# A fused cross-attention and FFN block of two layers: P turned by DMA in steps 75 to 123, and four orders changed

## What is computed

```python
x = x + tanh(g_xattn[0]) * attn(layernorm(x), ctx, mask, L0 weights)
x = x + tanh(g_ffn[0])   * mx_ffn(layernorm(x), w_gate, w_up, w_down)
x = x + tanh(g_xattn[1]) * attn(layernorm(x), ctx, mask, L1 weights)
x = x + tanh(g_ffn[1])   * (layernorm(x)[:, perm] @ dequant(w_packed, w_scales).T + bias)
# attn: q = rmsnorm(x @ Wq.T), k = rmsnorm(ctx @ Wk.T), v = ctx @ Wv.T   (per head)
#       softmax(q k.T / sqrt(128) + mask) @ v, then @ Wo.T
```

## Time and profile before

| | |
|---|---|
| median of three runs | 1327.74 us |
| the profiled execution, its own time | 1327.17 us |
| its span in the profile | 1325.3 us |
| TensorE busy | 1308.3 us (99%) |
| VectorE busy | 994.0 us (75%) |
| ScalarE busy | 864.3 us (65%) |
| GpSimd busy | 623.2 us (47%) |
| granted TensorE clock, mean | 1.00 |

### The profile page before, as it was taken

One profiled execution on the slowest core, in us unless ns is written; L12 is line 12 of the kernel. 1 busy time (PEld: TensorE's weight loads), 2 busy tenths in 40 slices (PEclk: granted clock), 3 DMA queues, 4 the chain that ended last, 5 costly groups with the idle time before them and its releaser, 6 DMA issues.

```text
span 1325.3 us, 25509 instructions
## 1 busy us (share of the span) xinstructions
PE 1308.3 (99%) x7497; PEld 1103.1 (83%) x7497; DVE 994.0 (75%) x2103; ACT 864.3 (65%) x3355; POOL 623.2 (47%) x683
## 2 busy tenths in 40 slices
PE   8999999999999999999999999999999999999998
PEld 7888888888888888877777788888888888888777
DVE  6878787887878788688878857686666767667776
ACT  5767667676767676645666556786666767666552
POOL 2546465555655666347677434532323333232222
PEclk9999999999999999999999999999999999999999
DMA  8011210212121110021310021423222221321111
GB/s 296 1 57 55 64 54 23 67 45 67 49 67 49 55 64 27 5 67 21 99 46 20 20 51 69 144 56 80 65 72 63 71 57 33 77 63 24 33 24 57
DMA packets 100877, 78.10 MB, mean 59 GB/s; under 512 B 70080, under 2 KB 91456, under 8 KB 96704
## 3 DMA queue, kind: packets, MB, share of 16 engines
q1 hardware_dynamic: 83808, 71.65, 18.6%
q10 hardware_dynamic: 16672, 4.46, 1.6%
q0 software_dynamic: 320, 1.05, 0.2%
HBM read 57.48 MB, written 3.15 MB: 46 GB/s over the span
## 4 chain that ended last, share of the span: by engine, by line
PE 88%; issue 5%; DVE 3%; POOL 1%; DMA 1%; ACT 1%; SPq 0%; POOLq 0%; ACTq 0%; DVEq 0%
PE bank L1286 62%; PE bank L1350 8%; PE bank L1278 7%; PE bank L1381 7%; PE bank L1312 2%; PE bank L1469 1%; PE bank L1367 1%; DMA p_turned<-p_planes 1%; POOL rstd L568 1%; DMA w_raw<-in_wv 1%; DVE probs L1122 0%; DVE pT_lo L1020 0%; ACT pT_hi L778 0%; DVE w_lo L892 0%; DVE p_whole L1015 0%
## 5 line engine op out<-in xcount | busy, mean ns | idle before, releaser
L539 POOL TENSOR_TENSOR w_lo<-w_raw,w_hi (+1 forms) x150 | 194.0, 1309 | 162.4 <-ACT w_hi L718 162.4
L757 ACT ACTIVATE squares<-bank 128x128 bf16<-128x128 f32 x512 | 134.8, 279 | 186.3 <-PE bank L1286 186.1
L1122 DVE SCALAR_TENSOR_TENSOR probs<-bank,mask_sb 128x512 f32<-128x512 f32 x127 | 87.6, 690 | 174.8 <-PE bank L1350 157.1
L699 ACT ACTIVATE probs<-probs,negmax 128x128 f32<-128x128 f32 x512 | 198.2, 392 | 5.4 <-DVE negmax L998 3.2
L564 POOL TENSOR_TENSOR meansq<-sumsq,scalars 128x5 f32<-128x5 f32 x128 | 27.5, 215 | 350.6 <-ACT squares L757 350.6
L568 POOL TENSOR_TENSOR rstd<-meansq,scalars 128x5 f32<-128x5 f32 x128 | 156.0, 1219 | 10.8 <-POOL meansq L564 1.1
L1286 PE MATMUL bank<-w_hi,oT_hi 128*128 (+1 forms) x512 | 150.9, 416 | 0.0
L1286 PE MATMUL bank<-w_hi,xT_hi 128*128 (+1 forms) x512 | 141.0, 396 | 0.2 <-ACT w_hi L668 0.2
L1286 PE MATMUL bank<-w_hi,oT_lo 128*128 (+1 forms) x512 | 137.9, 391 | 0.0
L1286 PE MATMUL bank<-w_lo,xT_hi 128*128 (+1 forms) x512 | 137.7, 390 | 0.1
L1286 PE MATMUL bank<-w_lo,oT_hi 128*128 (+1 forms) x512 | 137.7, 391 | 0.0
(11 more groups left out here) (129 smaller groups left out, 3002.3 us busy)
## 6 DMA issues: line engine op xcount, KB each, us to landing
w_raw<-in_wq SPq DMA_DIRECT2D x16, 1024.0 KB, 4.9
w_raw<-in_wo SPq DMA_DIRECT2D x16, 1024.0 KB, 4.9
fw_raw<-in_ffn_w SPq DMA_DIRECT2D x36, 192.0 KB, 2.3
w_raw<-in_wk SPq DMA_DIRECT2D x16, 256.0 KB, 5.3
w_raw<-in_wv SPq DMA_DIRECT2D x16, 256.0 KB, 5.6
x_sb<-in_x SPq DMA_DIRECT2D x7, 256.0 KB, 9.8
ctx_raw<-in_ctxT SPq DMA_DIRECT2D x7, 256.0 KB, 10.5
fw_raw<-in_ffn_w SPq DMA_DIRECT2D x7, 256.0 KB, 2.7
```

Source lines behind the costliest of these rows:

```text
L539: last = nc.gpsimd.tensor_tensor(lo, raw, hi.bitcast(FP32), ALU.subtract)
L699: last = nc.scalar.activation(probs[:, h * P:(h + 1) * P], probs[:, h * P:(h + 1) * P], ACT.Exp, bias=negmax[:, h:h + 1], accum_out=rowsum ...
L757: last = nc.scalar.activation(squares[:, h // 2, (b + 1) % 4, h % 2, :], q_bank(n, kind)[:, h * P:(h + 1) * P], ACT.Square, scale=SCALE, a ...
L1122: nc.vector.scalar_tensor_tensor(heads(probs[:, :]), heads(psSQ[:, :]), SCALE, mask_sb[:, :].unsqueeze(1).to_broadcast([P, REP, P]), ALU.m ...
```

## The change

It does seven things.

1. **Which steps turn P by DMA.** Steps 75 to 123 in place of 80 to 127 (`DMA0`, `DMA1`, `by_dma`, `turned_by_pe`). SyncE's loop starts with step 75; the loads of the next group stand between its transposes.
2. **VectorE's order in a DMA step.** `place_lower` stands ahead of the masked scores.
3. **`int4_weights`** stands in the middle of VectorE's steps 75 to 78, no longer at their end.
4. **`values()` in a down step** stands ahead of all 11 pieces of the hidden layer, no longer behind the eighth.
5. **`load_kv`** is one DMA of 4 KB per partition from an array `wkv` in which K's and V's weights lie side by side, so `loaded_qkv` counts 32 per group.
6. **Loads in the PLAIN loop.** SyncE waits for the transposes issued so far, issues `load_q`, then the first transpose of the group, then `load_kv`. Before, it issued `load_q` and `load_kv` without that wait, and then the transpose.
7. **The loads of group 10** are issued between the transposes of steps 75 to 79 (the weights of Q, K and V behind that of step 75, those of the output behind that of step 79).

```diff
-DMA0 = ZONE1 - BATCHES
+DMA0, DMA1 = ZONE1 - 13, LAST0 + 4
@@ by_dma, turned_by_pe
-            return kind == PLAIN or (isinstance(n, int) and DMA0 <= n < ALL)
+            return kind == PLAIN or (isinstance(n, int) and DMA0 <= n < DMA1)
-            return n - 1 - (ALL - DMA0 if isinstance(n, int) and n >= ALL else 0)
+            return n - 1 - (DMA1 - DMA0 if isinstance(n, int) and n >= DMA1 else 0)
@@ sync
             def load_kv(g, at, done):
-                for dram, part in ((wk, 0), (wv, 1)):
-                    dst = w_raw[:, at + WKV0:at + WO0].rearrange("p (k c n) -> p k c n", k=KT, c=2)[:, :, part, :]
-                    src = dram[bass.ds(g, 1)].rearrange("g p n -> p (g n)").rearrange("p (k n) -> p k n", k=KT)
-                    sp.dma_start(dst, src).then_inc(done, 16)
+                sp.dma_start(w_raw[:, at + WKV0:at + WO0], wkv[bass.ds(g, 1)].rearrange("g p n -> p (g n)")).then_inc(done, 16)
-            load_group(E, 0, None, step_of(C, BATCHES - 1) + 1)
+            freed = step_of(C, BATCHES - 1) + 1
@@ turning_group
                     if b == 0:
                         sp.wait_ge(kv_ps, before * BATCHES)
                         sp.wait_ge(q_ps, before * BATCHES)
+                        if not isinstance(before, int):
+                            sp.wait_ge(planes_turned, (before * BATCHES - DMA0) * 16)
                         load_q(g, at, loaded_qkv)
+                        if isinstance(before, int):
+                            load_kv(g, at, loaded_qkv)
+                    turn_probs(before * BATCHES + b)
+                    if b == 0 and not isinstance(before, int):
                         load_kv(g, at, loaded_qkv)
-                    turn_probs(before * BATCHES + b)
...
+            for n in range(DMA0, ZONE1 - BATCHES):
+                turn_probs(n)
+                if n == freed - 1:
+                    sp.wait_ge(kv_ps, freed)
+                    sp.wait_ge(q_ps, freed)
+                    load_q(E + 1, 0, loaded_qkv)
+                    load_kv(E + 1, 0, loaded_qkv)
+                if n == freed + 3:
+                    sp.wait_ge(y_ps, freed)
+                    load_wo(E + 1, 0, loaded_wo)
             turning_group(E + 1, 1)
-            for n in range(LAST0, ALL):
+            for n in range(LAST0, DMA1):
                 turn_probs(n)
@@ vector
+                if kind == ZONE and 0 <= n - INT4_0 < INT4_PARTS:
+                    int4_weights(n - INT4_0)
                 for k in gathered(n, kind):
...
+                if by_dma(n, kind):
+                    place_lower(n)
                 if has(n, 1):
 
                     dve.wait_ge(s_ps, n)
...
-                if by_dma(n, kind):
-                    place_lower(n)
                 if has(n, 1) and not qn_first(n, kind, t):
                     maximum(n)
...
-                if kind == ZONE and 0 <= n - INT4_0 < INT4_PARTS:
-                    int4_weights(n - INT4_0)
@@ tensor
-                if has(n, 2) and not by_dma(n, kind) and t.down is None:
+                if has(n, 2) and not by_dma(n, kind):
                     values()
...
                     for k, (r, rows) in enumerate(ITILES):
-                        if k == CHUNKS[2][0] // P:
-                            values()
```

More of the change, by code:

```diff
@@ L154, with flamingo_kernel @@
 NORM, SIX = sequences()
-def flamingo_kernel(nc, x, ctxT, mask, g_xattn, g_ffn, norms, wq, wk, wv, wo, ffn_w,
+def flamingo_kernel(nc, x, ctxT, mask, g_xattn, g_ffn, norms, wq, wkv, wo, ffn_w,
                     packedT, scalesT, perm, bias, w4_rows, out):
@@ L713, in split_upper @@
                     if k == 0:
-                        act.wait_ge(loaded_qkv, (j + 1) * 48)
+                        act.wait_ge(loaded_qkv, (j + 1) * 32)
                     if k == WO_PIECES[0]:
@@ L850, in _ @@
             ctx_upper(0)
-            act.wait_ge(loaded_kv0, 32)
+            act.wait_ge(loaded_kv0, 16)
             first_upper(KV_PIECES)
@@ L1532, in in_rows, with kv_rows @@
         return w.transpose(0, 3, 2, 1).reshape(GROUPS, P, KT * heads * P)
+    def kv_rows(k, v):
+        parts = [in_rows(w, 1).reshape(GROUPS, P, KT, 1, P) for w in (k, v)]
+        return np.concatenate(parts, axis=3).reshape(GROUPS, P, KT * 2 * P)
     def out_rows(w):
@@ L1556 @@
         "wq": np.concatenate([in_rows(L0_xattn_q_proj_w, REP), in_rows(L1_xattn_Wq, REP)]),
-        "wk": np.concatenate([in_rows(L0_xattn_k_proj_w, 1), in_rows(L1_xattn_Wk, 1)]),
-        "wv": np.concatenate([in_rows(L0_xattn_v_proj_w, 1), in_rows(L1_xattn_Wv, 1)]),
+        "wkv": np.concatenate([kv_rows(L0_xattn_k_proj_w, L0_xattn_v_proj_w), kv_rows(L1_xattn_Wk, L1_xattn_Wv)]),
         "wo": np.concatenate([out_rows(L0_xattn_o_proj_w), out_rows(L1_xattn_Wo)]),
```

## The result

| | before | after |
|---|---|---|
| median | 1327.26 us (4 runs, 1326.36 to 1328.62) | 1319.15 us (4 runs, 1318.69 to 1320.3) |
| profiled execution | 1327.17 us | 1320.3 us |
| its span | 1325.3 us | 1318.5 us |
| TensorE busy | 1308.3 us | 1302.9 us |

The ratio is 0.9943, with a 95% interval of 0.993 to 0.9955: faster by 8.1 us, where 11.9 was forecast. The direction and the range held, in part because errors cancelled: a term that was set at +0.3 measured +4.0, and the PLAIN loop with steps 120 to 123 gained 2.0 more than forecast. The profiled execution, 1320.3 us, is the slowest of the four, so its stretches show less gain (6.8 us) than the median does.

A forecast was written before the change was run, and what follows sets the result against it. TensorE, busy 99% of the span, was taken as the bound, with small stalls to remove. The terms summed to -11.9 us from 1327.17, so 1315.3 profiled and a median of 1316; 8-in-10 range 1311.5 to 1322.5.

The forecast's parts named there:

- start: Kernel start: one load issue in place of two brings the first K/V product earlier; -1.0 us, at most 1.3.
- down and gate steps, 57 to 74: Seven down steps: values() ahead of all pieces fills TensorE's wait; 0.6 us for six, 0.3 for one, -3.9.
- steps 75 to 79: Five steps lose four TensorE transposes each, -2.25 us, less 0.25 charged for VectorE and GpSimd interference: -2.0.
- steps 80 to 87: Written-out steps already turning P by DMA: no such stall there, so no gain.
- PLAIN and 120 to 123: PLAIN loop: place_lower ahead of the mask ends the wait for pT_lo, 9.17 to 9.08 us over 32 steps; -2.8.
- 124 to the end: Steps 124 to 127: turning P on TensorE costs +1.8 but removes waits on VectorE's copy; -2.5 us in all.
- Loads and late transposes: DMA transposes landing late, with loads queued between them: taken as +0.3 us, with 1.7 either way.
- Rival 1: Down and last steps: freed waits are taken by the next ones, such as the third chunk's DMA; 1322 us, chance 0.14.
- On turning a tile through TensorE: Rival 2, steps 75 to 79 and PLAIN: P by DMA and the new order gain nothing; 1321 us, chance 0.10.
- Rival 3: Over 49 steps: the transpose lands late in every step; slower from a mean landing of 3.85 us, chance 0.04.

The follow-up runs named there:

- before_kv: The kernel before the change with only load_kv made one DMA, all else as it was; measured 1327.18 us, ratio 1.0003.
- spread102: The changed kernel with 102 already met waits added, six in each of steps 57 to 73 of TensorE's list; measured 1315.99 us, ratio 0.9916.
- from76: The changed kernel with 64 already met waits in steps 57 to 72 and P turned by DMA only from step 76; measured 1318.65 us, ratio 0.9946.
- lower_back: The changed kernel with place_lower behind the masked scores again in all DMA steps; measured 1323.31 us, ratio 0.9977.
- dma_127: The changed kernel with steps 124 to 127 turning P by DMA as well, as before; measured 1320.94 us, ratio 0.9956.

## Why the prediction came out as it did

Two profiles, stretch by stretch; the cost of the late transposes is taken out of each and stands in a row of its own. The column on the right has the second profile of the changed kernel (after_again, span 1316.5).

| term | forecast | profile | | second profile |
|---|---|---|---|---|
| start | -1.0 | -0.57 | | -0.5 |
| step 51 | 0 | +0.98 | not in the forecast | -0.2 |
| down and gate steps, 57 to 74 | -3.9 | -2.21 | | -2.5 |
| steps 75 to 79 | -2.0 | -1.21 | | -1.2 |
| steps 80 to 87 | 0 | -0.03 | | 0.0 |
| PLAIN and 120 to 123 | -2.8 | -4.75 | | -4.7 |
| 124 to the end | -2.5 | -3.05 | | -3.1 |
| late transposes | +0.3 | +4.04 | 6.11 - 2.07 | +3.4 |
| sum | -11.9 | -6.80 | 1318.5 - 1325.3 | -8.8 |

**The step that failed** is "Loads and late transposes". I wrote "I take +0.3, with 1.7 either way", and had seen one late transpose, with no cause for it. A late one costs 0.87 (6.11 / 7), near the 0.74 of the forecast; what was wrong is their number, seven where there had been two (six in the second profile). The cause that I lacked is the fetch. The "five more transposes in the written-out code" are not the reason: of the seven only that of step 77 is one of them. The other six (80, 82, 84, 91, 93, 122) were turned by DMA before too; the changed list puts TensorE's fetches elsewhere in these steps.

Two sums of the prediction are off as well: its best ends add up to -15.6 (not -15.8), its worst to +4.1 (not +3.0). The forecast itself does not hang on them.

**Start.** The bound of 1.3 held, the -1.0 did not: what I had put down as a risk came. The first tiles of context and x, issued by ScalarE, land later:

```profile
x_sb<-in_x ACTq DMA_DIRECT2D x1, 256.0 KB, 4.4
ctx_raw<-in_ctxT ACTq DMA_DIRECT2D x1, 256.0 KB, 6.0
```

The kernel before had 2.7 and 4.2, and the profiles agree: the first tile of x takes 2.7 to 3.0 in the two with the old `load_kv`, 4.1 to 4.5 in the twelve with the new one. So the warm-up comes later (timeline), and the first product starts straight behind it, at 9.89:

```profile
7.64 0.66 PE L1290 MATMUL bank<-ident,f_s 128*128 128x128 f32 x4 [1.29 <-DVE f_s L891]
...
8.14 1.91 PE L1507 MATMUL bank<-ident 128*128 128x128 f32 x16
...
9.89 0.71 PE L1298 MATMUL bank<-w_hi,ctx_hi 128*128 128x256 f32 x4
```

The -0.57 is no more than the spread of one kernel: in the second profile the first product starts at 11.19, and step 8 starts at 82.2 to 83.1 in the profiles with the new `load_kv` and no increments, at 82.7 and 83.0 in those with the old one. before_kv found no gain in the time. So this term may be nothing.

**Step 51** lasted 10.74; in the thirteen other profiles it lasted 9.51 to 9.91. ScalarE waited a microsecond longer for the output weights (2.33 us, 1.27 before). A q8 packet started with that load's issue (491.45 and 491.40); but in the second profile one did so too (491.55 and 491.49), and the step lasted 9.52. The cause stays open.

**Down steps.** Five of the seven gained 0.54 to 0.55 (0.6 was forecast), step 70 0.35, and the wait of the earlier trace rows is gone. Four gate steps gave back 0.14 to 0.17 each, 0.6 in all, for VectorE's `f_q`, whose work is no shorter. And steps 66 and 67 gained nothing. In step 66 the third chunk landed late, as it had before the change (3.98 us there, 4.28 now):

```profile
686.45 0.82 PE L1479 MATMUL bank<-wT,f_iqT 128*128 128x512 bf16 x3 [1.25 <-DMA f_iqT<-f_iq]
```

It was issued at 682.12, more than 4 us before, with a q8 packet at 684.2; where no fetch came (spread102) the step lasted 13.79, not 15.19. But then step 67 lasted 14.43, not 13.15: the pair lasts 28.2 to 28.4 us in all fourteen profiles, early chunk or late, new order or old. What holds it there is another wait. In spread102 (timeline: VectorE, GpSimd, TensorE's weight loads):

```profile
683.50 2.52 POOL L551 TENSOR_TENSOR w_lo<-w_raw,w_hi 128x512 fp32r<-128x512 f32 x2
...
684.29 0.51 DVE L969 TENSOR_SCALAR amax<-amax 128x16 f32<-128x16 f32 x1
684.84 1.21 DVE L971 TENSOR_SCALAR inv_pow<-amax 128x16 uint32<-128x16 uint32 x1
...
698.62 0.55 PEld L1330 LDWEIGHTS bank<-wT,f_xqT 128*128 128x128 bf16 x4 [1.43 <-DVE f_q L975]
```

Two small operations of VectorE that take 0.17 each a pair of steps earlier take 0.51 and 1.21 beside GpSimd's split of weights, and end with it (686.0); 1.4 us later than usual in its step VectorE goes on, and TensorE waits for `f_q`. That the split stretches them is read from these times and was not tested. Rival 1 was right in kind, since the freed waits were taken by the next ones, and took 1.7 of the 2.9 that it gave to these steps; but the next ones were VectorE's `f_q` more than the chunk.

**Steps 75 to 79.** Four of the five gained 0.47, as counted (77 once its fetch is set aside). Step 75 lasts 10.1 to 10.2 in every kernel that starts there, with a landing of 3.1: its transpose is issued 3.5 us into the step and not 1.9, because ScalarE's exponentials end 1.6 us into it (in step 76 they end ahead of the step), and the planes wait for them. from76, where the first transpose by DMA in step 76 costs nothing of the kind, shows that it is the step and not the switch. The moved `int4_weights` and GpSimd's split cost nothing there.

**PLAIN.** More than forecast: 9.05 and not 9.08, and the two steps at each end of a group lost a stall too (9.37 to 9.39 and 9.20 to 9.29, now 9.08 to 9.12). lower_back, 3.8 slower in time, confirms the size.

**Steps 124 and on.** 125 came at 10.14 (forecast 10.25). 124 stayed at 10.73 (forecast 10.25), since TensorE waits 0.46 us for the layer norm's tile (`f_s`) there. The mechanism was half right: dma_127 shows that 1.3 of the 3.1 came with the order, which I had counted only as PLAIN's.

**Rivals.** On turning a tile through TensorE the rows decided: for DMA in PLAIN, for TensorE only behind step 124. Rival 3, a transpose late in every step, never came near (median landing 3.0), but its mechanism is the one that hurt, in seven steps.

The Trainium skill, "Runtime: NRT & Kernel Launch", section "Instruction fetch mechanics", says that an engine's instructions come in blocks of 16 KiB (256 instructions) by a DMA queue of its own while it executes, at a cost that is "mostly hidden". The trace agrees on the size (packets of 16,384 bytes) and on the spacing (nine packets from step 75 to 93, so eight gaps in 18.1 steps, 2.26 steps each; a step has 109 matmuls and weight loads and, by an estimate, some five waits, which makes 258). It disagrees on the cost for a kernel that waits for a small DMA in each step: 0.25 to 1.2 us for each of the seven late steps.

## What to carry to other kernels

Where a step waits for a DMA with little slack (here 0.6 us), look at the instruction queues beside it: one 16 KB fetch beside it added 0.7 to 1.8 us to that DMA. Any edit to the busiest engine's list, even one far away, moves the fetches, so compare two versions with the late steps counted apart, or a lucky edit is taken for a good one. Cheap instructions in front, put where matmuls cover them, show how much of a time is this luck. And before a wait is blamed for a long step, add up the steps beside it: steps 66 and 67 traded some 1.3 us between them, and their sum stayed within 0.2.

## What was not expected of the hardware

- A transpose by DMA of 3.0 us takes 3.8 to 4.9 when a 16 KB instruction packet starts 0.6 to 2.9 us behind its issue (62 of 64). None that started ahead of the issue made it late.
- In the loops only the first pass fetches: the changed kernel has no q8 packet between 139.1 and 468.1 us, nor between 959.8 and 1202.2 us, and no PLAIN step from 96 on had a late transpose in any profile.
- A semaphore increment ahead of TensorE's idle list costs 0.165 us; a wait already met between matmuls of 0.23 us costs nothing that shows.
- The place of a fetch is not a fixed count of instructions: 30 more moved one fetch by 1.1 us and another by 5.6, and the same kernel's fetch moved by 1.4 between two executions. Why is open.
